# Attention score stacks filled to 64 rows a half, and the weighing of a unit in five steps of 256 columns

## The reference

```python
x = L0_attn_x                                   # (8, 512, 256)
# attention, on layernorm(x)
qkv = xn @ W_qkv + b_qkv                        # 16 heads of 16
scores = einsum('bhqd,bhkd->bhqk', q, k) * 16 ** -0.5
attn = softmax(where(causal, -inf, scores))
x = x + einsum('bhqk,bhkd->bhqd', attn, v) @ W_out + b_out
# experts, on layernorm(layernorm(x)) * gamma + beta
probs = softmax(xn @ gate_w); w, idx = top_k(probs, 2); w = w / sum(w)
h = gelu(xn @ w1[e] + b1[e]); out_e = h @ w2[e] + b2[e]
x = x_normed_once + sum_e w_e * out_e + x
```

## Time and profile before

| | us |
|---|---|
| median of 3 runs | 976.07 |
| lowest, highest | 970.33, 979.5 |
| span of the profiled execution | 991.0 |
| PE busy | 872.7 |
| DVE busy | 722.9 |
| ACT busy | 587.6 |
| POOL busy | 461.7 |

### The profile page before, as it was taken

The page is one execution under the profiler, slowest core; times in us unless marked ns, Lnnn a source line. Parts: engine busy times, 40 slices in busy tenths (PEclk is TensorE's granted clock), DMA queues, the critical chain, the costliest instruction groups (busy, mean ns, idle before and its releaser), DMA issues.

```text
span 991.0 us, 21222 instructions
## 1 busy us (share of the span) xinstructions
PE 872.7 (88%) x6870; PEld 576.0 (58%) x6870; DVE 722.9 (73%) x1658; ACT 587.6 (59%) x1079; POOL 461.7 (47%) x561
## 2 busy tenths in 40 slices
PE   4999988787788888897878898989989999999996
PEld 3655422242433434352424686879869989989875
DVE  6578878758578797969893785885766766666664
ACT  2776566656678686858776562554544455445453
POOL 2000123334425747655667546574476464544441
PEclk9999977876887978677987997999989999999998
DMA  9988667654857676575727452242223232323231
GB/s 213 293 275 256 207 180 220 177 139 120 215 168 225 172 189 183 159 191 150 201 77 232 125 120 39 46 85 51 47 36 54 50 49 46 56 50 50 36 52 19
DMA packets 146327, 130.09 MB, mean 131 GB/s; under 512 B 59344, under 2 KB 128848, under 8 KB 146096
## 3 DMA queue, kind: packets, MB, share of 16 engines
q1 hardware_dynamic: 115648, 87.51, 31.8%
q0 software_dynamic: 15680, 18.95, 12.0%
q10 hardware_dynamic: 14896, 22.28, 7.1%
HBM read 83.63 MB, written 44.80 MB: 130 GB/s over the span
## 4 chain that ended last, share of the span: by engine, by line
PE 49%; DVE 17%; issue 10%; DMA 9%; POOL 6%; SPq 5%; ACT 3%; POOLq 1%; ACTq 0%; another core or an unknown queue 0%; DVEq 0%
PE banks L769 15%; PE banks L787 14%; PE banks L582 4%; PE banks L697 3%; PE banks L685 3%; DVE arena L1230 3%; PE banks L641 2%; PE banks L572 2%; DVE weights L1384 2%; DMA weighed_values<-arena 2%; POOL out L1702 2%; DVE arena L1232 2%; POOL slot_tokens L1649 2%; PE banks L626 2%; DMA inverse_sums<-arena 2%
## 5 line engine op out<-in xcount | busy, mean ns | idle before, releaser
L991 ACT ACTIVATE arena<-banks,arena 128x256 f32<-128x256 f32 (+1 forms) x312 | 152.2, 541 | 192.9 <-issue 126.8
L769 PE MATMUL banks<-arena,weights 128*128 128x256 f16 (+1 forms) x1872 | 207.4, 266 | 11.5 <-issue 8.6
L787 PE MATMUL banks<-weights,arena 128*128 x1704 | 197.5, 275 | 3.6 <-DVE arena L1514 2.6
L769 PEld LDWEIGHTS banks<-arena,weights 128*128 x1872 | 174.0, 98 | 39.5 <-issue 16.2
L1702 POOL DMA_INDIRECT out<-arena x71 | 115.6, 1628 | 168.4 <-DVE arena L1525 131.8
L787 PEld LDWEIGHTS banks<-weights,arena 128*128 128x128 f16 x1704 | 166.4, 99 | 26.9 <-issue 6.4
L641 PE MATMUL banks<-arena 50*128 50x128 f16 (+3 forms) x512 | 126.4, 352 | 37.9 <-DMA arena<-arena 12.2
L1512 DVE TENSOR_SCALAR arena<-arena 128x512 f16<-128x512 f32 (+1 forms) x156 | 77.1, 494 | 70.6 <-ACT arena L991 58.9
L613 PE MATMUL banks<-arena 48*128 48x384 f16 (+3 forms) x512 | 103.1, 345 | 26.4 <-DVE arena L1233 9.3
L1514 DVE SCALAR_TENSOR_TENSOR arena<-arena 128x512 f16<-128x512 f32 (+1 forms) x156 | 111.0, 711 | 5.6
L641 PEld LDWEIGHTS banks<-arena 50*128 50x128 f16 x512 | 39.1, 102 | 128.7 <-issue 43.3
(11 more groups left out here) (190 smaller groups left out, 1338.9 us busy)
## 6 DMA issues: line engine op xcount, KB each, us to landing
weights<-in_L_ffn_w ACTq DMA_DIRECT2D x16, 1024.0 KB, 7.8
arena<-in_L_ffn_w SPq DMA_DIRECT2D x32, 512.0 KB
qk_parts<-weights SPq DMA_DIRECT2D x64, 128.0 KB
arena<-qk_parts SPq DMA_DIRECT2D x128, 64.0 KB, 3.2
weighed_values<-arena SPq DMA_DIRECT2D x32, 256.0 KB
token_rows<-arena SPq DMA_DIRECT2D x12, 512.0 KB, 4.3
arena<-qk_parts SPq DMA_DIRECT2D x128, 32.0 KB, 3.3
arena<-weighed_values SPq DMA_DIRECT2D x32, 128.0 KB
```

What stands on the lines that cost most here:

```text
L769: m = pe.matmul(bank[:, c * TILE:c * TILE + WIDTH[j]], w1[:, k, wp, f:f + P], xp[:, k, 0:WIDTH[j]], start=(i == 0), stop=(i == len(terms) ...
L787: m = pe.matmul(bank[:, c * D:(c + 1) * D], hp[:, f, c * P:(c + 1) * P], w2[:, f // (FC // 2), wp, f % (FC // 2), :], start=(f == 0 and i ...
L991: m = act.activation(h_32[r % 2][:, c, 0:WIDTH[j]], banks[:, 1 + c2, c * TILE:c * TILE + WIDTH[j]], ACT.Gelu, bias=b1_now[j % 2][:, 2 * c2 ...
```

## The change

The first part concerns rows. The two rows of the maxima move from rows 48 and 49 of a half to its last two, 62 and 63. `maxima_scores` now reads 62 rows instead of 48, and `scores_T` reads 64 instead of 50. The rows between are zero in q, by four more memsets on POOL at the start, so they add nothing to a score.

The second part concerns the weighing. A unit is weighed in five steps of 4 matmuls with 256 columns. The fourth step is made of two key tiles with 128 columns, so it has 8 matmuls. The steps stand behind each of the five combos instead of behind the first four. `copy_o`, `keep_o` and `move_o` move by 7, 4 and 2 ticks. The exponentials, which overwrite the probabilities of the unit two before, wait for the step that read that key tile and not for the whole unit.

```diff
+    TOPS_AT = HALF_ROWS - TOPS
...
-        W_ORDER = (0, 3, 1, 2)
+        W_STEPS = (((0, 0, 256),), ((0, 256, 512),), ((1, 0, 256),), ((1, 256, 384), (3, 0, 128)), ((2, 0, 256),))
+        W_ALL = len(W_STEPS)
+        W_READ = {0: 2, 1: 4, 3: 4, 2: 5}
...
-            for i, kt in enumerate(W_ORDER):
-                at(after + (6, 16, 24, 34)[i], "weigh", (u, kt))
-            at(after + 41, "copy_o", u)
+            last = u == UNITS - 1
+            for i in range(W_ALL):
+                at(after + ((6, 13, 20, 27, 34) if last else (6, 15, 24, 33, 43))[i], "weigh", (u, i))
+            at(after + (41 if last else 48), "copy_o", u)
...
-            at(after + 51, "keep_o", u)
-            at(after + (84 if late else 70), "move_o", u)
+            at(after + (51 if last else 55), "keep_o", u)
+            at(after + (84 if late else 72), "move_o", u)
...
-                half = slice(HALF_ROWS * j, HALF_ROWS * j + STACK)
+                half = slice(HALF_ROWS * j, HALF_ROWS * j + TOPS_AT)
...
-                half = slice(HALF_ROWS * j, HALF_ROWS * j + STACK + TOPS)
+                half = slice(HALF_ROWS * j, HALF_ROWS * j + HALF_ROWS)
...
-                for h in range(HG):
-                    a, width = PT_AT[kt], T - kt * P
-                    m = pe.matmul(banks[32 * h:32 * h + 32, O_BANK, kt * P:T], v_and_ones(u, kt, h),
-                                  p_T[u % 2][:, h, a:a + width], start=(kt == W_ORDER[0]), stop=(kt == W_ORDER[-1]),
-                                  tile_position=(0, 32 * h))
+                for kt, first_col, end_col in W_STEPS[step]:
+                    for h in range(HG):
+                        m = pe.matmul(banks[32 * h:32 * h + 32, O_BANK, kt * P + first_col:kt * P + end_col],
+                                      v_and_ones(u, kt, h), p_T[u % 2][:, h, PT_AT[kt] + first_col:PT_AT[kt] + end_col],
+                                      start=(step == 0), stop=(step == W_ALL - 1),
+                                      tile_position=(0, 32 * h), skip_group_check=True)
...
-                        w.wait_ge(sem("weighed"), TT * (u - 1))
+                        w.wait_ge(sem("weighed"), W_ALL * (u - 2) + max(W_READ[kt] for _, kt, _ in blocks))
...
             for s in range(4):
+                g.memset(q_st[s], 0.0)
                 m = g.memset(k_st[s], float(2 ** SHIFT))
...
-                    row, first_row, n = HALF_ROWS * j + STACK, TOPS * j * HQ * TT, TOPS * HQ * TT
+                    row, first_row, n = HALF_ROWS * j + TOPS_AT, TOPS * j * HQ * TT, TOPS * HQ * TT
```

More of the change, by code:

```diff
@@ L672, in top_turn, with weigh @@
                 turn_tops(bank).then_inc(sem("side_made"), 1)
-            def weigh(u, kt):
-                w.wait_ge(sem("masked"), 3 * u + (3 if kt == 2 else 2))
-                if kt == W_ORDER[0]:
+            def weigh(u, step):
+                w.wait_ge(sem("masked"), 3 * u + (3 if step == W_ALL - 1 else 2))
+                if step == 0:
                     w.wait_ge(sem("ones_set"), 1)
@@ L886, in exponentials @@
                 for s in range(2):
+                    j, blocks = E_USES[2 * i + s]
                     if u >= 2:
-                        w.wait_ge(sem("weighed"), TT * (u - 1))
+                        w.wait_ge(sem("weighed"), W_ALL * (u - 2) + max(W_READ[kt] for _, kt, _ in blocks))
                     else:
                         w.wait_ge(sem("tops"), 2 * 2 * LATE)
-                    j, blocks = E_USES[2 * i + s]
                     w.wait_ge(sem("scored_T"), exp_use(u, 2 * i + s) + 1)
@@ L908, in copy_o @@
             def copy_o(u):
-                w.wait_ge(sem("weighed"), TT * (u + 1))
+                w.wait_ge(sem("weighed"), W_ALL * (u + 1))
                 if u > 0:
@@ L968, in load_late @@
             def load_late(i, e_, m_, k_):
-                w.wait_ge(sem("weighed"), TT * (UNITS - 1))
+                w.wait_ge(sem("weighed"), W_ALL * (UNITS - 1))
                 w.wait_ge(sem("w_stored"), 32 * LENT)
@@ L1509, in split_hidden @@
                 else:
-                    w.wait_ge(sem("weighed"), TT * UNITS)
+                    w.wait_ge(sem("weighed"), W_ALL * UNITS)
                 pair, width = slice(2 * c2, 2 * c2 + 2), slice(0, WIDTH[j])
@@ L1785, in load_v @@
                 if u >= 2:
-                    w.wait_ge(sem("weighed"), TT * (u - 1))
+                    w.wait_ge(sem("weighed"), W_ALL * (u - 1))
                 w.wait_ge(sem(f"v_store{b % 2}"), 16 * (b // 2 + 1))
```

## The result

The change made the kernel a little slower. Over 20 runs each the median is 975.01 us (967.88 to 982.08) against 971.90 us of before (962.09 to 979.5), and the ratio is 1.0049, 95% interval 1.0027 to 1.0070. That is +4.8 us where -15 was forecast, and the time lies inside the stated range (940 to 982) only because the range was wide. The forecast of 961 us also stood on the median of three runs, 976.07 us, and the 20 runs of before have 971.90.

A forecast was written before the change was run, and what follows sets the result against it. SP was taken to bound the first five or six attention units, PE and DVE in turns later. Terms -20 (clock), +3 (steps), -2 (smaller step), +3 (SP's order), +1 (copy) sum to -15: 976 to 961 us, range 940 to 982.

The forecast's parts named there:

- The clock, -20 us: Attention: fuller rows in the score matmuls bring PE's fast clock back sooner and hold it longer, saving 20 us.
- a third less time at the slow level (56 us): Attention: of 169 us at 1.2 GHz on PE, the added rows remove a third, 56 us.
- the price of 0.36 us for each slow microsecond: Attention: each microsecond at 1.2 GHz lengthens the kernel 0.36 us, taken between 0.59 and 0.22 from two unit pairs.
- SP's order, +3: SP's queue: load of v goes ahead of the store, so `move_o` waits 0.5 us longer in some six units, +3 us.
- the rival that ended slower: SP becomes the bound at `move_o`: swap and later copy cost 14 to 22 us in some 20 units; chance 0.15.
- that sign: SP's waits at `move_o`: some 3 to 6 us more in total; 40 or more would mean SP is the bound.
- Five steps, +3: Weighing on PE: a fifth step adds 0.25 us a unit, up to 0.25 more for the second tile; +3 us.
- the copy, +1: ACT's copy of the weighed values waits for a step behind the last combo, mostly covered; +1 us.
- the smaller first step, -2: Weighing: a first step of 256 columns ahead of the transpose of the maxima shortens ACT's wait; -2 us.
- The memsets, 0: Start of kernel, POOL: four new memsets finish by some 20 us, before the first transfer needing them at 33.10; 0 us.
- The first rival: Attention: the clock does not care about rows, so that gain is gone; 967 to 981 us, chance 0.30.
- The test I had named for the first term: Attention window: mean clock near 0.87 in place of 0.80; at 0.80 or 0.81 the clock gain and forecast are wrong.

The follow-up runs named there:

- e1: Only the rows (62 and 64 a half), weighing and timetable as in the kernel before; ratio 0.9984 to the kernel before.
- e2: Only the five steps and new ticks, including SP's swapped order, with 48 and 50 rows, against the kernel before; ratio 1.0080.
- e6: Kernel before with the second and third key tile weighed for 128 query columns only (896 of 1280 columns a unit); ratio 1.0030.
- e14: Kernel before with the change's rows and part of the maxima left out on DVE (half the columns in three of five slots); ratio 0.9848.
- e4: Kernel before with only the load of v moved ahead of the store of the weighed values in SP's queue; ratio 1.0034.
- e3: Whole change with only the load of v put back behind the store of the weighed values in SP's queue; ratio 0.9997 to the kernel before.
- e5: Five steps and their ticks with 48 and 50 rows, load of v behind the store, against the kernel before; ratio 1.0005.
- e0: Kernel before, unchanged, run again for a second profile; ratio 0.9981, span 965.5 us.
- e15: Kernel before with part of the maxima left out on DVE (half the columns in three of five slots); ratio 0.9893.
- e8: Kernel before with the reading back of weighed values moved from tick 70 to 94, inversion and its store also later; ratio 1.0178.
- e9: Kernel before with the change's rows and the reading back moved from tick 70 to 94, inversion and its store later; ratio 1.0151.

## Why the prediction was wrong

**The clock, -20 us.** This term failed, and with it the forecast. It was a product of two numbers. The first, a third less time at the slow level (56 us), was somewhat high: 41 us by e1, and by e2 all of it comes from the rows, none from the even steps. The step that failed is the second, the price of 0.36 us for each slow microsecond: by e1 it is 1.5 / 41 = 0.04, and 4.5 / 41 = 0.11 at most. I had read it from pairs of units of the same kind that differed in their clock, and they differed in more than that. In the second pair DVE is busy for 12.22 of 12.61 us and for 14.23 of 14.64, with 34 and 38 instructions: it had 2.01 us more to do, and the unit was 2.03 us longer, so nothing is left there for the clock. PE was even idle for less of the slower unit, 1.5 us against 2.6. In the first pair PE is busy nearly throughout, so the clock may have a part, but POOL had 13.48 us to do in place of 5.44. What one slow microsecond costs can't be read from such pairs. PE's time in attention is worth little, though three of its lines have a fifth of the chain of waits. How little is open: e6 can't tell, and 19.0 us less of it gave 4.4 us in e14. That a faster PE waits for things that come no sooner fits these runs, but was not tested by itself. I had the rows for a doubt, DVE 326.3 us busy against PE's 348.6 in attention and the chain without a leader, and I used a correlation in place of it.

**SP's order, +3.** Mechanism and sign were right, and the size was too small. It measured +3.3 in the kernel before (e4), 5 in the whole change (e3 against it) and 7 with the steps alone (e5 against e2). I had counted six units; after the change SP waited for the store 21 times, against 15 in e0. This is the mechanism of the rival that ended slower, without its size: I gave that one 14 to 22 us and made it depend on 40 us of SP's waits at `move_o`. Counted as I did, at the line of `move_o` alone, they went from 25.0 (30.4 in e0) to 35.6, so that sign did not come. But the count left out the waits at L47, and with them it is 54.6, and 39.8 without the change.

**Five steps, +3; the copy, +1; the smaller first step, -2.** Together +2, and e5 gives 0.5, with an interval of -2.3 to 3.3, so these terms may well have been right. In PE's own time the 0.25 us a step was exact: five times 0.67. The second tile, which I had at up to 0.25, costs 0. On the path it can't be told from nothing. The weighing was busy 121.4 us and not 130 or more, because the clock rose: it is 130.0 us in e5, with the steps and the clock of before. ACT's wait for the transpose fell as foreseen, and that too gave nothing one can see.

**The memsets, 0.** Nothing contradicts it: e1, which has them, is not slower than before, and in the trace of after all eight are done at 18.7 us, while the first transfer that waits for them starts at 35.4.

**The sum by the measured terms**: -1.5 for the rows and +7.8 for the steps with SP's swap make +6.3, against +4.8 (2.6 to 6.8) for both.

The first rival, no gain from the clock, was nearest: right in that next to nothing is gained, wrong in its reason, as the clock did rise. The test I had named for the first term, a mean clock near 0.87 or at least over 0.81, would have come out half right at 0.84, with the forecast still wrong. It tested the clock and not what the clock is worth.

What stays open is how much of the 1.5 us is real, and whether the clock would pay with DVE relieved (e14 against e15, 4.4 us, intervals overlapping). Shown are a quarter for each microsecond of DVE, at most 0.11 for each microsecond at the slow level in the kernel before, and 17 us for reading back 24 ticks later with the inversion moved along. Which part of that round trip holds the rest was not taken apart.

## What to carry to other kernels

Before a faster clock or a shorter step on one engine is priced, change that alone and see whether the time moves; stretches of one trace that differ in their clock differ in the work of other engines too. Taking work from TensorE is a blunt test, since its clock may fall and keep it busy for as long (e6): look at its busy time, and not only at the work. When a timetable is stretched for one engine, list what changes places on each transfer queue: here one load that went ahead of a store cost more than all else the change did. And take a second profile of the same kernel before arguing from one stretch of it.

## What the hardware showed that I had not expected

Rows of zeros in a matmul raised TensorE's clock. Going from 48 and 50 rows to 62 and 64, where the added rows of q are all zero, the mean granted clock of the run went from 0.907 to 0.928 (11 runs, deviation 0.004 between runs; before 34 runs, 0.005), with the same columns and the same count of matmuls. In two more pairs it was 0.907 to 0.929 (e15 against e14) and 0.889 to 0.905 (e8 against e9). The prediction had guessed at this from one window, which e0 did not repeat; it is e1 that shows it. Only q is zero in these rows, k holds 8192 there; q is streamed in `scores_T` and is the stationary operand in `maxima_scores`, and no run tells which of the two matmuls does it. And the reverse: with 384 of 1280 weighing columns left out it fell from 0.901 to 0.873 (e6).
